# Attention's scaling of z ahead of its addition to x, with two buffers for the scaled z

## The chip, the cores and the metric

The kernel runs on one core of one Trainium2 chip, as one program. The metric is the device time of one execution in microseconds; the median of 3 runs is given. Engines are named as in the profile: PE is TensorE (PEld its weight loads), DVE is VectorE, ACT is ScalarE, POOL is GpSimd, SP is the engine whose queue issues the DMAs (SPq).

## What is computed

A block of three layers on x of 16 x 1024 x 256 in float32: half an FFN with weights and activations quantised to FP4 in blocks of 16, linear attention with 16 heads, and the same half FFN again.

```python
x = x + 0.5 * ffn(layernorm(x), w_gate, w_up, w_down)
x = x + attn(layernorm(x), Wqkv, bqkv, Wout, bout, gamma, beta)
x = x + 0.5 * ffn(layernorm(x), w_gate, w_up, w_down)

# in attn, after q, k, v: causal linear attention through cumulative sums
num = einsum('blhe,blhef->blhf', q, cumsum(k v)); den = einsum('blhe,blhe->blh', q, cumsum(k)) + eps
z = (num / den) @ Wout.T + bout
return (z - mean(z)) / sqrt(var(z) + 1e-5) * gamma + beta
```

The change touches the last line and the addition of its result to x.

## The kernel before

x stays in SBUF (x_sb) for the whole kernel, as N = 128 tiles of 128 rows (partitions) by 256 columns. Three stages pass over the tiles: the first FFN, attention, and the second FFN. Each engine has a program of its own, and they meet only through semaphores: `ready(engine, name, t)` waits until the step called name is done for tile t, `freed(...)` until a buffer's last reader is done. Each engine issues its instructions strictly in the order in which the step function writes them. In all stages the work is skewed: in step i an engine works on several tiles at once, each at another point of its way. The order of work on an engine is thus written out by hand, and nothing reorders it.

Attention is run for steps i = -4 to 131. Steps 5 to 120 are a loop on each engine, whose body holds four steps (`ATTN_TURN = 4`), so 29 passes. The first steps are interleaved with the first FFN's last, the last ones with the second FFN's first.

What one step of attention does, as far as it matters here (names are those in the trace, with their line):

- TensorE: q and k (ps_qk, L1265) of tile i+1 from xT, a transpose of k (L1273), v (L1278), the numerator of tile i-1 (ps_num, L1297 and L1302), the scores of tile i (L1310), the sums k v of tile i (L1321), and the projection z of tile i-2 (ps_z; L1330 the bias, L1333 the rest). ps_z has one buffer: L1330 waits for z_gamma, the increment of zg.
- VectorE: statistics of x for tile i+4 (L1053) and of z for tile i-3 (L1059), the masked scores (L1063), the two aggregations (L1072 for z, L1074 for x, both into mv), the addition to x for tile i-4 (L1079), the state before (L1085), zg for tile i-3 (L1091: z less its mean, times gamma), den (L1095, waits for num), feat (L1099), the reciprocal (L1102), o (L1108), and the states second and first (L1113, L1120).
- GpSimd: k_eo (L1148, L1149, waits for feat), the lower half of o (L1153, o_split), the state mid (L1160), the lower half of the normalised x (L1164), 1/sqrt of both variances (L1175 adds eps, L1177 is the power -0.5, on two columns: one for x, one for z; L1175 waits for both aggregations), the shift (L1181), and beta added to x_sb (L1183).
- ScalarE: among others the upper half of o (L1192) and the normalised x (L1240, L1244).
- SP: it issues oT's transpose (L1034) after o_split and then xT's transpose (L1040) after x_split, always in this order; xT feeds L1265 two steps later on its tile.

So the addition of tile i-4 uses the zg that VectorE wrote in the step before. zg is one buffer of 128x256 float32 at 13376 bytes into the stage area. z's 1/sqrt(var) comes from GpSimd between the two.

In the first FFN two lines serve below as a measure: L714 on VectorE (128x16, reads two tensors in SBUF) and L791 on GpSimd (128x704, reads SBUF).

Of the kernel before, what the change touches and what calls it, by code (L numbers as in the profile page):

```python
# [31 lines left out]
ALU = mybir.AluOpType  # L32
# [4 lines left out]
P = 128  # L37
D = 256
# [31 lines left out]
def column(ap, t):  # L70
    return ap[:, bass.ds(t, 1)]


def valid(t, n):
    return not isinstance(t, int) or 0 <= t < n
# [45 lines left out]
def macaron(nc, x, wqkv, bqkv, wout, bout, gamma, beta, wg, wu, wd, out):  # L121
# [6 lines left out]
    with ExitStack() as whole:  # L128
# [27 lines left out]
        def at(name, offset, shape, dt=F32):  # L156
# [9 lines left out]
        of_ffn_0, of_ffn_1 = [ffn(nc, ffn_sems, attn_sems, at, N, half, x_sb, x_t, out_t, wgu_hi, wgu_lo, wd_hi, wd_lo, unscale,  # L166
                                  minus_half, eps, minus_one, offsets, x_loaded, attn_added, stored) for half in range(2)]
        of_attn_steps = attention(nc, attn_sems, at, N, x_sb, A, ident, minus_half, eps, ffn_sems, attn_added, sem("attn_set_up"))
        block = whole.enter_context(nc.Block())

# [740 lines left out]
def attention_constants(sbuf, N):  # L911
    def sb(name, shape, dt=F32):
# [5 lines left out]
                     sb("feat_eps", [P, 1]), sb("keep", [P, N]))  # L918


ATTN_PLACES = {"o": 8352, "oT": (1024, 2048), "o_hl": (9376, 4096), "mid": (5632, 6176), "before": (6720, 7264), "first": 7808, "second": 11264, "k_nat": 12352, "zg": 13376,
               "k_eo": (15104, 17152), "scores": 19200, "v_nat": (23296, 24384), "v_eo": (25472, 27648), "q_feat": (29824, 30848), "q_rows": (31872, 33920),
               "expo": (35968, 38016), "xT": (40064, 41088), "x_hl": (42112, 43136), "xn": 44160,
               "bn6": 45184, "z_bn6": 45216, "mv": (45248, 45280), "rstd": (45376, 45408), "shift": (45440, 45472),
# [3 lines left out]
def attention(nc, S, at, N, x_sb, A, ident, minus_half, eps, F, attn_added, set_up):  # L928
    unscale, o_scale, one, rows, causal, diag, even, odd, of_pair, of_pair_eps, eps2, own, ones3, bout3, feat_eps, keep = (
        A.unscale, A.o_scale, A.one, A.rows, A.causal, A.diag, A.even, A.odd, A.of_pair, A.of_pair_eps, A.eps2, A.own, A.ones3, A.bout3, A.feat_eps, A.keep)  # L930
    with ExitStack() as scope:
        def sb(name, shape, dt=F32):
            return at("attn_" + name, ATTN_PLACES[name], shape, dt)

        def pair(name, shape, dt=F32):
            return [at(f"attn_{name}{j}", ATTN_PLACES[name][j], shape, dt) for j in range(2)]

        def psum(name, shape, dt=F32):
            return scope.enter_context(nc.psum_tensor("attn_" + name, shape, dt))
# [3 lines left out]
        mv = pair("mv", [P, 4])  # L943
        rstd = pair("rstd", [P, 2])
# [8 lines left out]
        k_nat = sb("k_nat", [P, D])  # L953
# [5 lines left out]
        first, second = sb("first", [P, DC, PAIRS, VW]), sb("second", [P, DC, PAIRS, VW])  # L959
        mid = pair("mid", [P, DC, PAIRS, VW])  # L960
        before = pair("before", [P, DC, PAIRS, VW])
        den, rden = sb("den", [P, HEADS]), sb("rden", [P, HEADS])
        o = sb("o", [P, D])
        o_hl = pair("o_hl", [P, 2 * D], F16)
        oT = pair("oT", [P, 2 * DC, P], F16)
        z_bn6 = sb("z_bn6", [P, 6])
        zg = sb("zg", [P, D])

        ps_qk = psum("ps_qk", [P, 2 * DC, P])
        ps_kT_first = psum("ps_kT_first", [P, 512])  # L970
# [3 lines left out]
        ps_z = psum("ps_z", [P, 512])  # L974

        def ready(eng, name, t, k=1, per=1):
            eng.wait_ge(S[name], t * per + k)
# [23 lines left out]
        def by_head(ap):  # L1001
            return ap.rearrange("p c k w -> p (c k) w")
# [40 lines left out]
        def vector_step(dve, i, par):  # L1043
            oth = 1 - par
            ts, tf, tm, tz, ta = i + 4, i + 1, i - 1, i - 3, i - 4
# [26 lines left out]
                nc.vector.bn_aggr(mv[oth][:, 2:4], z_bn6[:]).then_inc(S["z_stats"], 1)  # L1072
            if valid(ts, N):
                nc.vector.bn_aggr(mv[par][:, 0:2], bn6[:]).then_inc(S["stats"], 1)  # L1074
            if valid(ta, N):
                ready(dve, "x_beta", ta)
                dve.wait_ge(S["rstd"], ta + 7)
                ready(dve, "z_gamma", ta)
                nc.vector.scalar_tensor_tensor(x_sb[:, ta, :], zg[:], rstd[par][:, 1:2], x_sb[:, ta, :], ALU.mult, ALU.add).then_inc(attn_added, 1)  # L1079
            if valid(i, N) and not (isinstance(i, int) and i == 0):  # L1080

                ready(dve, "mid", tm)
                ready(dve, "kv_second", tm)
                freed(dve, "num_done", i, 2)
                nc.vector.scalar_tensor_tensor(by_head(before[par][:]), by_head(mid[oth][:]), column(keep, i), by_head(second[:]), ALU.mult, ALU.add).then_inc(S["before"], 1)  # L1085
            if valid(tz, N):

                ready(dve, "z_stats", tz)
                if valid(ta, N):
                    dve.wait_ge(attn_added, ta + 1)  # L1090
                nc.vector.scalar_tensor_tensor(zg[:], ps_z[:, 0:D], mv[oth][:, 2:3], rows[:, 1, :], ALU.subtract, ALU.mult).then_inc(S["z_gamma"], 1)  # L1091
            if valid(tm, N):

                ready(dve, "num_done", tm)
# [156 lines left out]
        def tensor_step(pe, i, par):  # L1251
# [72 lines left out]
            if valid(to, N):  # L1324
# [9 lines left out]
                last.then_inc(S["proj_done"], 1)  # L1334

        return Programs(sync_step, vector_step, gpsimd_step, scalar_step, tensor_step)


# [208 lines left out]
```

## Time and profile before

| | |
|---|---|
| median of 3 runs | 2185.19 us (2185.08 to 2187.68) |
| profiled execution, its own time | 2185.49 us |
| its span, first to last instruction | 2183.1 us |
| mean granted TensorE clock | 0.994 |
| busy, share of the span | PE 96%, DVE 94%, ACT 88%, POOL 87% |
| attention's loop | about 800 to 1410 us of the span |

Busy shares are averages over stages. Matmuls are pipelined and their ends are modelled in the trace, so short stalls of TensorE are better seen from the times at which its steps begin than from its busy time. "Idle before <-releaser" says who let an engine go on.

### The profile page before, as it was taken

To read this page: it belongs to the slowest core of one execution; us is meant where nothing else is said; L and a number is where in the kernel's file an instruction comes from. 1 tells how busy PE (TensorE), PEld (TensorE's weight loads), DVE (VectorE), ACT (ScalarE), POOL (GpSimd) and SP (SyncE) were. 2 spreads that over 40 slices of the span, in tenths; PEclk is the share of its full clock that TensorE was granted. 3 is DMA by queue.
4 is the path that set the end of the run, shared out by engine and by line. 5 is a ranking of instruction groups with operands and counts; after the bars stand their busy time and mean duration, and the time that the engine had idled before them with its cause. 6 is when DMAs were issued, how large, how long until landed. Compare 5 with 4: busy or idle time off the path is not lost.

```text
span 2183.1 us, 90488 instructions
## 1 busy us (share of the span) xinstructions
PE 2100.8 (96%) x30384; PEld 1503.3 (69%) x30384; DVE 2044.3 (94%) x5231; ACT 1926.2 (88%) x4136; POOL 1907.3 (87%) x3002
## 2 busy tenths in 40 slices
PE   3899999999999999999999999969999999999998
PEld 1566666666666688888888888855666666666665
DVE  7999999999999789999999999979999999999997
ACT  7888888888888789999999999978988888888885
POOL 5999999999999778888888888868999999999996
PEclk9999999999999999999999999989999999999999
DMA  4665555555555432222232222224555555555555
GB/s 103 131 125 115 116 115 116 115 115 115 114 114 108 84 58 61 61 61 61 61 62 62 61 61 61 62 44 76 120 116 114 114 114 114 114 115 115 115 118 118
DMA packets 719855, 208.72 MB, mean 96 GB/s; under 512 B 666400, under 2 KB 719520, under 8 KB 719776
## 3 DMA queue, kind: packets, MB, share of 16 engines
q1 hardware_dynamic: 719776, 207.76, 46.6%
q8 instruction: 39, 0.64, 0.1%
q14 instruction: 40, 0.33, 0.1%
HBM read 20.38 MB, written 16.78 MB: 17 GB/s over the span
## 4 chain that ended last, share of the span: by engine, by line
PE 89%; issue 3%; POOL 3%; DVE 3%; DMA 1%; ACT 1%; SPq 1%; POOLq 0%; DVEq 0%; ACTq 0%
PE ffn_ps_gu L861 39%; PE ffn_ps_down L873 20%; PE attn_ps_qk L1265 8%; PE attn_ps_sc L1310 5%; PE attn_ps_num L1297 4%; PE attn_ps_v_second L1278 4%; PE attn_ps_z L1333 3%; PE attn_ps_num L1302 2%; PE attn_ps_kT_first L1273 1%; PE attn_ps_z L1330 1%; PE attn_ps_kT_first L1321 1%; DMA attn_xT<-attn_x_hl 1%; POOL ffn_h_hl L791 1%; DMA x_sb<-in_L_ffn_w_up 0%; POOL ffn_h_hl L792 0%
## 5 line engine op out<-in xcount | busy, mean ns | idle before, releaser
L861 PE MATMUL ffn_ps_gu<-wgu_hi,ffn_xT 128*128 128x512 f16 (+1 forms) x3072 | 737.7, 363 | 18.4 <-DVE ffn_hx L710 8.0
L861 PEld LDWEIGHTS ffn_ps_gu<-wgu_hi,ffn_xT 128*128 128x128 f16 x3072 | 300.7, 98 | 304.7 <-issue 22.3
L861 PE MATMUL ffn_ps_gu<-wgu_lo,ffn_xT 128*128 128x512 f16 (+1 forms) x1536 | 431.0, 362 | 0.0
L791 POOL TENSOR_TENSOR ffn_h_hl<-ffn_q,ffn_h_scale_hi 128x704 f16<-128x704 f16 x256 | 352.4, 1376 | 28.0 <-DVE ffn_q L751 8.6
L807 ACT ACTIVATE ffn_quarter<-ffn_y,offsets 128x960 int16<-128x960 f32 (+2 forms) x264 | 282.5, 1070 | 99.3 <-DVE ffn_y L759 96.9
L873 PE MATMUL ffn_ps_down<-wd_hi,ffn_hT 128*128 128x256 f16 x2816 | 349.3, 273 | 8.1 <-DVE x_sb L735 4.2
L792 POOL TENSOR_TENSOR ffn_h_hl<-ffn_q,ffn_h_scale_lo 128x704 f16<-128x704 f16 x256 | 355.1, 1387 | 0.0
L873 PEld LDWEIGHTS ffn_ps_down<-wd_hi,ffn_hT 128*128 128x128 f16 x2816 | 274.6, 98 | 68.8 <-issue 7.1
L721 DVE TENSOR_REDUCE ffn_per_block<-ffn_hx 128x60 f32<-128x960 f32 (+2 forms) x264 | 298.1, 1129 | 5.3
L759 DVE TENSOR_TENSOR ffn_y<-ffn_hx,ffn_per_block 128x960 f32<-128x960 f32 (+2 forms) x264 | 292.6, 1108 | 0.0
L843 ACT ACTIVATE ffn_odd<-ffn_quarter,offsets 128x960 f16<-128x960 int16 (+2 forms) x264 | 278.8, 1056 | 10.8 <-POOL ffn_shift L786 10.8
L802 ACT ACTIVATE ffn_silu<-ffn_ps_gu,unscale 128x704 f32<-128x704 f32 x256 | 215.5, 842 | 73.6 <-PE ffn_ps_gu L861 71.5
L861 PEld LDWEIGHTS ffn_ps_gu<-wgu_lo,ffn_xT 128*128 128x128 f16 x1536 | 150.7, 98 | 155.0 <-issue 1.9
L710 DVE SCALAR_TENSOR_TENSOR ffn_hx<-ffn_ps_gu,unscale,ffn_silu 128x704 f32<-128x704 f32 x256 | 240.9, 941 | 17.0 <-PE ffn_ps_gu L861 13.3
L777 POOL TENSOR_TENSOR ffn_x_hl<-ffn_q,ffn_x_scale_hi 128x256 f16<-128x256 f16 x256 | 158.1, 617 | 73.4 <-DVE ffn_q L751 59.4
L873 PE MATMUL ffn_ps_down<-wd_lo,ffn_hT 128*128 128x256 f16 x1536 | 209.5, 273 | 0.0
L1265 PE MATMUL attn_ps_qk<-attn_xT,attn_w_hi 128*128 128x128 f16 x2048 | 178.8, 219 | 8.0 <-DMA attn_xT<-attn_x_hl 5.4
L873 PEld LDWEIGHTS ffn_ps_down<-wd_lo,ffn_hT 128*128 128x128 f16 x1536 | 150.3, 98 | 17.4
L782 POOL TENSOR_TENSOR ffn_x_hl<-ffn_q,ffn_x_scale_lo 128x256 f16<-128x256 f16 x256 | 161.6, 631 | 0.0
L1063 DVE TENSOR_TENSOR attn_scores<-attn_ps_sc,attn_causal 128x1024 f32<-128x1024 f32 x128 | 154.3, 1205 | 0.0
L845 ACT ACTIVATE ffn_hx<-x_sb,ffn_shift,ffn_rstd 128x256 f32 (+1 forms) x256 | 150.0, 586 | 1.5 <-POOL ffn_shift L786 1.5
L1265 PEld LDWEIGHTS attn_ps_qk<-attn_xT,attn_w_hi 128*128 128x128 f16 x2048 | 136.0, 98 | 22.2 <-DMA attn_xT<-attn_x_hl 16.8
(184 smaller groups left out, 5246.3 us busy)
## 6 DMA issues: line engine op xcount, KB each, us to landing
x_sb<-in_L_attn_x SPq DMA_DIRECT2D x128, 128.0 KB, 2.4
out<-x_sb SPq DMA_DIRECT2D x128, 128.0 KB, 2.1
attn_v_eo<-attn_v_nat SPq DMA_DIRECT2D x256, 34.0 KB, 1.8
ffn_xT<-ffn_x_hl SPq DMA_TRANSPOSE x256, 2.5
ffn_hT<-ffn_h_hl SPq DMA_TRANSPOSE x256, 3.5
attn_xT<-attn_x_hl SPq DMA_TRANSPOSE x128, 2.4
attn_oT<-attn_o_hl SPq DMA_TRANSPOSE x128, 2.5
x_sb<-in_L_ffn_w_gate SPq DMA_DIRECT2D x2, 352.0 KB, 5.0
```

The costliest lines, as they stand in the source:

```text
L710: nc.vector.scalar_tensor_tensor(hx[par][:, 0:INNER], ps_gu[par][:, INNER:2 * INNER], unscale[:, 1:2], silu[:], ALU.mult, ALU.mult).then_i ...
L721: nc.vector.tensor_reduce(amax[:, blocks_in(front)], blocks(hx[par][:, front]), AXX, ALU.max, apply_absolute_value=True).then_inc(S["amax" ...
L759: nc.vector.tensor_tensor(blocks(y[:, front]), blocks(hx[par][:, front]), over_block(inv[:, at], at.stop - at.start), ALU.mult).then_inc(S ...
L782: nc.gpsimd.tensor_tensor(blocks(x_hl[par][:, D:]), blocks(q[par][:, INNER:]), over_block(x_scale_lo[par][:], XB), ALU.mult).then_inc(S["x ...
L791: nc.gpsimd.tensor_tensor(blocks(h_hl[par][:, 0:INNER]), blocks(q[par][:, 0:INNER]), over_block(h_scale_hi[par][:], HB), ALU.mult)
L792: nc.gpsimd.tensor_tensor(blocks(h_hl[par][:, INNER:]), blocks(q[par][:, 0:INNER]), over_block(h_scale_lo[par][:], HB), ALU.mult).then_inc ...
L802: nc.scalar.activation(silu[:], ps_gu[par][:, 0:INNER], ACT.Silu, scale=unscale[:, 0:1]).then_inc(S["silu"], 1)
L807: nc.scalar.activation(quarter[:, back], y[:, back], ACT.Identity, bias=offsets[:, 0:1], scale=4.0 / HALF_MIN).then_inc(S["quarter"], 1)
L843: nc.scalar.activation(odd[:, back], quarter[:, back], ACT.Identity, bias=offsets[:, 1:2], scale=HALF_MIN / 4.0).then_inc(S["odd"], 1)
L861: last = nc.tensor.matmul(ps_gu[par][:, a:b], xT[par][:, c, :], w[:, k, a:b], start=(n == 0), stop=(n == len(terms) - 1))
L873: last = nc.tensor.matmul(ps_down[:, 0:D], hT[par][:, c, :], w[:, c, :], start=(n == 0), stop=(n == len(terms) - 1))
L1265: last = nc.tensor.matmul(ps_qk[:, col, :], w[:, col, k], aT, start=(n == 0), stop=(n == len(terms) - 1))
```

## The change

zg becomes a pair of buffers. The instruction that writes it (L1091) moves ahead of the addition (L1079) and of before (L1085). In step i it writes `zg[oth]`, and the addition reads `zg[par]`, which the step before wrote. Two waits go: the addition's for z_gamma, and zg's for the addition (attn_added). No instruction is added or dropped. The second buffer lies at 3072 bytes, in space that attention didn't use. Lines behind the place have numbers that are 3 lower in the changed kernel; zg becomes L1078, the addition L1082, before L1088.

```diff
-ATTN_PLACES = {..., "zg": 13376,
+ATTN_PLACES = {..., "zg": (13376, 3072),
...
-        zg = sb("zg", [P, D])
+        zg = pair("zg", [P, D])
...
                 nc.vector.bn_aggr(mv[par][:, 0:2], bn6[:]).then_inc(S["stats"], 1)
+            if valid(tz, N):
+
+                ready(dve, "z_stats", tz)
+                nc.vector.scalar_tensor_tensor(zg[oth][:], ps_z[:, 0:D], mv[oth][:, 2:3], rows[:, 1, :], ALU.subtract, ALU.mult).then_inc(S["z_gamma"], 1)
             if valid(ta, N):
                 ready(dve, "x_beta", ta)
                 dve.wait_ge(S["rstd"], ta + 7)
-                ready(dve, "z_gamma", ta)
-                nc.vector.scalar_tensor_tensor(x_sb[:, ta, :], zg[:], rstd[par][:, 1:2], x_sb[:, ta, :], ALU.mult, ALU.add).then_inc(attn_added, 1)
+                nc.vector.scalar_tensor_tensor(x_sb[:, ta, :], zg[par][:], rstd[par][:, 1:2], x_sb[:, ta, :], ALU.mult, ALU.add).then_inc(attn_added, 1)
             if valid(i, N) and not (isinstance(i, int) and i == 0):
                 ...
                 nc.vector.scalar_tensor_tensor(by_head(before[par][:]), ...).then_inc(S["before"], 1)
-            if valid(tz, N):
-
-                ready(dve, "z_stats", tz)
-                if valid(ta, N):
-                    dve.wait_ge(attn_added, ta + 1)
-                nc.vector.scalar_tensor_tensor(zg[:], ps_z[:, 0:D], mv[oth][:, 2:3], rows[:, 1, :], ALU.subtract, ALU.mult).then_inc(S["z_gamma"], 1)
```

VectorE's order in one of the four steps of attention's loop, before (the numbers behind names are the program's buffers):

```order
L1074 BN_AGGR attn_mv_136<-attn_bn_135 128x2
L1079 ISA [waits attn_z_gamma,attn_rstd,attn_x_beta]
L1079 SCALAR_TENSOR_TENSOR x_sb<-attn_zg,attn_rstd_138,x_sb 128x256
L1085 SCALAR_TENSOR_TENSOR attn_before_165<-attn_mid_164,attn_keep,attn_second 128x136 [waits attn_num_done,attn_kv_second,attn_mid]
L1091 SCALAR_TENSOR_TENSOR attn_zg<-attn_ps_z,attn_mv_137,attn_rows 128x256 [waits attn_added,attn_z_stats]
L1095 TENSOR_SCALAR attn_den<-attn_ps_num,attn_o_scale 128x16 [waits attn_num_done]
```

And the same step in the changed kernel:

```order
L1074 BN_AGGR attn_mv_136<-attn_bn_135 128x2
L1078 SCALAR_TENSOR_TENSOR attn_zg_176<-attn_ps_z,attn_mv_137,attn_rows 128x256 [waits attn_z_stats]
L1082 ISA [waits attn_rstd,attn_x_beta]
L1082 SCALAR_TENSOR_TENSOR x_sb<-attn_zg_175,attn_rstd_138,x_sb 128x256
L1088 SCALAR_TENSOR_TENSOR attn_before_165<-attn_mid_164,attn_keep,attn_second 128x136 [waits attn_num_done,attn_kv_second,attn_mid]
L1092 TENSOR_SCALAR attn_den<-attn_ps_num,attn_o_scale 128x16 [waits attn_num_done]
```

zg has moved up by two operations, its only wait is the one for the aggregation, and den now follows before. The other engines' orders are the same in both kernels.

## Rows read from the trace of the kernel before

**Rows 1.** The page, busy us (share of the span) x instructions

```profile
PE 2100.8 (96%) x30384; PEld 1503.3 (69%) x30384; DVE 2044.3 (94%) x5231; ACT 1926.2 (88%) x4136; POOL 1907.3 (87%) x3002
```

**Rows 2.** Windows: stretch, length, busy by engine, granted clock, DMA share, GB/s

```profile
820.00:1410.00 590.00, 588.47 (x18183) 526.38 (x18180) 542.08 (x1522) 571.58 (x1305) 506.48 (x978) 1.00 0.30 61
```

**Rows 3.** Waits, 820 to 1410 us: us in total, times, longest

```profile
PEld attn_ps_qk L1265 <- DMA attn_xT<-attn_x_hl: 7.4, 27, 0.3
...
DVE attn_den L1095 <- PE attn_ps_num L1302: 39.4, 109, 0.5
...
POOL attn_k_eo L1148 <- DVE attn_expo L1099: 15.8, 53, 0.3
```

**Rows 4.** Timeline of weight loads: start, us, instruction, idle before

```profile
1110.64 0.29 PEld L1265 LDWEIGHTS attn_ps_qk<-attn_xT,attn_w_hi 128*128 128x128 f16 x4
...
1115.40 0.10 PEld L1330 LDWEIGHTS attn_ps_z<-attn_bout,attn_ones 128*128 128x128 bf16 x1
...
1116.13 0.26 PEld L1265 LDWEIGHTS attn_ps_qk<-attn_xT,attn_w_hi 128*128 128x128 f16 x4
...
1121.63 0.23 PEld L1265 LDWEIGHTS attn_ps_qk<-attn_xT,attn_w_hi 128*128 128x128 f16 x4 [0.28 <-DMA attn_xT<-attn_x_hl]
...
1132.36 0.25 PEld L1265 LDWEIGHTS attn_ps_qk<-attn_xT,attn_w_hi 128*128 128x128 f16 x4
```

**Rows 5.** Timeline of SP's queue, step k1

```profile
1117.67 1.20 SPq L1034 DMA_TRANSPOSE attn_oT<-attn_o_hl  x1
1119.13 1.19 SPq L1040 DMA_TRANSPOSE attn_xT<-attn_x_hl  x1
```

**Rows 6.** Timeline of GpSimd, step k0 into k1

```profile
1113.32 0.27 POOL L1175 TENSOR_TENSOR attn_rstd<-attn_mv,attn_eps 128x2 f32<-128x2 f32 x1 [0.29 <-DVE attn_mv L1072]
1113.67 0.70 POOL L1177 TENSOR_TENSOR attn_rstd<-attn_rstd,minus_half 128x2 f32<-128x2 f32 x1
...
1114.80 0.73 POOL L1183 TENSOR_TENSOR x_sb<-x_sb,attn_rows 128x256 f32 x1
1115.63 0.48 POOL L1148 TENSOR_SCALAR attn_k_eo<-attn_expo,attn_even 128x256 f32<-128x256 f32 x1
1116.20 0.48 POOL L1149 TENSOR_SCALAR attn_k_eo<-attn_expo,attn_odd 128x256 f32<-128x256 f32 x1
1116.77 0.67 POOL L1153 TENSOR_TENSOR attn_o_hl<-attn_o,attn_o_hl 128x256 f16<-128x256 f32 x1
```

**Rows 7.** Timeline of VectorE, step k0

```profile
1112.93 0.17 DVE L1072 BATCH_NORM_AGGREGATE attn_mv<-attn_z_bn 128x2 f32<-128x6 f32 x1
...
1113.08 0.45 DVE L1079 SCALAR_TENSOR_TENSOR x_sb<-attn_zg,attn_rstd,x_sb 128x256 f32 x1
1113.45 0.35 DVE L1085 SCALAR_TENSOR_TENSOR attn_before<-attn_mid,attn_keep,attn_second 128x136 f32<-128x136 f32 x1
1113.73 0.48 DVE L1091 SCALAR_TENSOR_TENSOR attn_zg<-attn_ps_z,attn_mv,attn_rows 128x256 f32<-128x256 f32 x1
1114.43 0.23 DVE L1095 TENSOR_SCALAR attn_den<-attn_ps_num,attn_o_scale 128x16 f32<-128x16 f32 x1 [0.23 <-PE attn_ps_num L1302]
...
1115.24 0.24 DVE L1102 RECIPROCAL attn_rden<-attn_den 128x16 f32<-128x16 f32 x1
1115.51 0.42 DVE L1108 TENSOR_TENSOR attn_o<-attn_ps_num,attn_rden 128x256 f32<-128x256 f32 x1
```

**Rows 8.** Timeline of ScalarE, step k1

```profile
1116.20 0.40 ACT L1192 ACTIVATE attn_o_hl<-attn_o 128x256 f16<-128x256 f32 x1
```

**Rows 9.** Timeline of GpSimd in attention's first steps, no addition beside it

```profile
770.99 0.19 POOL L1175 TENSOR_TENSOR attn_rstd<-attn_mv,attn_eps 128x2 f32<-128x2 f32 x1
771.26 0.71 POOL L1177 TENSOR_TENSOR attn_rstd<-attn_rstd,minus_half 128x2 f32<-128x2 f32 x1
```

**Rows 10.** Timelines of VectorE and GpSimd in the first FFN, two places

```profile
549.03 0.17 DVE L714 TENSOR_TENSOR ffn_x_scale_lo<-ffn_scale,ffn_x_scale_hi 128x16 f32<-128x16 f32 x1
...
549.02 1.41 POOL L791 TENSOR_TENSOR ffn_h_hl<-ffn_q,ffn_h_scale_hi 128x704 f16<-128x704 f16 x1
...
695.74 1.38 DVE L714 TENSOR_TENSOR ffn_x_scale_lo<-ffn_scale,ffn_x_scale_hi 128x16 f32<-128x16 f32 x1
...
695.72 1.38 POOL L791 TENSOR_TENSOR ffn_h_hl<-ffn_q,ffn_h_scale_hi 128x704 f16<-128x704 f16 x1
```

**Rows 11.** Timeline of VectorE in attention's last steps

```profile
1467.20 0.48 DVE L1079 SCALAR_TENSOR_TENSOR x_sb<-attn_zg,attn_rstd,x_sb 128x256 f32<-128x256 f32 x1
1467.79 0.48 DVE L1091 SCALAR_TENSOR_TENSOR attn_zg<-attn_ps_z,attn_mv,attn_rows 128x256 f32<-128x256 f32 x1
```

More of the change, by code:

```diff
@@ L918, in attention_constants @@
                      sb("feat_eps", [P, 1]), sb("keep", [P, N]))
-ATTN_PLACES = {"o": 8352, "oT": (1024, 2048), "o_hl": (9376, 4096), "mid": (5632, 6176), "before": (6720, 7264), "first": 7808, "second": 11264, "k_nat": 12352, "zg": 13376,
+ATTN_PLACES = {"o": 8352, "oT": (1024, 2048), "o_hl": (9376, 4096), "mid": (5632, 6176), "before": (6720, 7264), "first": 7808, "second": 11264, "k_nat": 12352, "zg": (13376, 3072),
                "k_eo": (15104, 17152), "scores": 19200, "v_nat": (23296, 24384), "v_eo": (25472, 27648), "q_feat": (29824, 30848), "q_rows": (31872, 33920),
```

## Prediction

> **What bounds the kernel now.** I read the page's busy line first: TensorE is busy for 96% of the span [rows 1]. Then the stage that the change touches, attention's loop, in a row of the windows view: from 820 to 1410 us TensorE is busy for 588.5 of 590 us at a granted clock of 1.00, so at 2.4 GHz [rows 2]. That busy time hides stalls, as the times of the steps show. One pass of the loop on every engine does four tiles ("a turn", steps k0 to k3), and there are 29 turns. In the timeline of weight loads k0 begins at 1110.64, k1 at 1116.13 and k2 at 1121.63, and the next k0 at 1132.36: 21.72 us a turn, 5.43 a step [rows 4]. Ahead of k2 the loads stood 0.28 us for the transpose that makes xT; the view of waits counts 27 of these, 7.4 us, one in each turn [rows 2 to 4]. So once a turn TensorE is bound by whoever makes xT late.
>
> Follow it back. k2's xT was issued on SP at 1119.13, right behind oT's, which began at 1117.67 and keeps SP until 1118.87 [rows 5]. oT waits for GpSimd's o_split (L1153), which ran from 1116.77 to 1117.44 [rows 6]. ScalarE's half of it was ready at 1116.60, earlier than GpSimd's own last operation, which ended at 1116.68 [rows 6, 8]. So GpSimd held it up. GpSimd runs without a wait from 1113.32 on, where L1175 starts once VectorE has written the statistics: L1175, L1177 (the power), the shift, L1183, then k_eo at 1115.63, 0.10 after L1183's end and so not waiting for VectorE's feat [rows 6]. **What GpSimd loses between 1113.32 and 1115.6 in k0, TensorE loses at k2**, once in each turn.
>
> VectorE is not the bound here: before each den (L1095) it waits for TensorE's num, 39.4 us over 109 times, 0.23 us of it in this k0 [rows 3, 7].
>
> **The change, part by part.** No instruction is added or dropped. Three things happen.
>
> (1) zg (L1091, 0.48 us) goes ahead of the addition (L1079) and of before (L1085). It also frees ps_z for TensorE sooner, but that frees nothing: in k0 zg ended at 1114.21, and the bias matmul that waits for it loads at 1115.40 [rows 4, 7]. Price 0.
>
> (2) The wait of zg for the addition goes, and the addition's wait for zg is now on one of the step before. Neither wait was a stall in the loop, since before lay between them: it is 1113.45 to 1113.80, and zg starts at 1113.73 [rows 7]. What comes instead is a wait of zg for the statistics of L1072, which end at 1113.10 [rows 7]. For a VectorE operation that waits for the last one the rows show a start 0.03 us behind its end (L1102 ends at 1115.48, L1108 starts at 1115.51) [rows 7], and at the most 0.11 (the addition ends at 1467.68, zg starts at 1467.79) [rows 11]. I take 0.03: zg's new wait is the only one on it, and the 0.11 stood behind two. So zg starts at 1113.13, where the addition started at 1113.08: 0.05 us longer a step, and 0.13 at most. The idle 0.23 before den takes either [rows 7]. Price 0 for VectorE; without that idle it would be 128 times 0.05, 6.4 us.
>
> (3) The addition moves past GpSimd's L1175 and onto L1177. This is what I price, since the two engines exclude each other. In the first FFN, VectorE's L714, which takes 0.17 us, started 0.02 us after GpSimd's L791 and then took 1.38, as long as L791 itself. Where it started only 0.01 after, it took 0.17 and L791 took 1.41 rather than 1.38 [rows 10]. So the first to start has it (up to 0.01 us apart VectorE wins), and the other waits. L714 reads two tensors in SBUF; so do the addition (zg, x_sb) and before (mid, second). zg reads PSUM and one tensor in SBUF. Now look at L1175 in k0: the addition ends at 1113.53 and L1175 at 1113.59, 0.27 long, where the same operation with no addition beside it took 0.19 [rows 6, 7, 9]. So the addition gives way 0.13 us ahead of its recorded end (1113.59 less 0.19 is 1113.40), and L1175 had lost 0.08.
>
> The Trainium skill has this as a rule, in "SBUF — State Buffer", section "Who interferes with whom": a VectorE instruction with two SBUF inputs and a GpSimd instruction that reads SBUF keep each other out for the whole instruction, by order of start. The rows agree but for the end: held to the addition's full end, the sum below would be 0.31 us a turn, 9.0 over the loop.
>
> After the change, in k0: L1175 starts at 1113.32 as before, is free, and ends at 1113.51. L1177 follows L1175's start by 0.27 when free (770.99, 771.26) [rows 9], so it starts at 1113.59. zg, from 1113.13, takes 0.48, and the next operation starts 0.08 ahead of an end (before, 0.35 long, to zg: 1113.45 to 1113.73) [rows 7]: the addition starts at 1113.53, 0.06 us ahead of L1177, and so goes first. It takes 0.45 when nothing holds it [rows 7], ends at 1113.98 and gives way at 1113.85. L1177's own 0.70 (0.71 when nothing was near) [rows 6, 9] then ends at 1114.55, where it ended at 1114.37: **0.18 us later**. All that follows on GpSimd up to o_split moves by it, and k2's xT wait goes from 0.28 to 0.46. In k1 the same clash puts L1177 at one place relative to the statistics, so the delay isn't added a second time; in about half the steps (53 of them, 15.8 us) GpSimd waits for VectorE's feat at k_eo anyway, 0.3 us a time, and the delay goes into that [rows 3].
>
> Sum: 29 turns by 0.18 is 5.2 us. The last few steps of attention outside the loop have the same two operations and GpSimd on the chain; three by 0.18, 0.5 us, is an estimate. Together 5.7. The profiled execution took 2185.49 (2183.1 of span and 2.4 around it), 0.3 above the median of 2185.19; from the median it is 2190.9.
>
> **The rivals.** (a) *GpSimd's power comes first.* If zg's wait costs 0.11, the addition starts at 1113.61, 0.02 behind L1177's 1113.59, and by L714's rows that is late enough. L1177 gets in, ends at 1114.29, 0.08 earlier than now, and k2's wait shrinks: 29 by 0.08, 2.3 us less, 2182.9. ScalarE's half, ready at 1116.60, would not allow more than about 0.1 [rows 8]. For it: a lead of only 0.06 in the forecast. Against it: the single wait. This one is not slower. Chance 0.12.
>
> (b) *zg's wait costs nothing*, since L1074 runs between: zg starts at 1113.08 where the addition did. Then all comes 0.05 earlier, the delay is 0.13, and 32 of them are 4.2: 2189.4. Against it: waiting operations start 0.03 behind an end, others 0.08 ahead of it [rows 7]. Chance 0.10. The Trainium skill says so in "VectorE: DVE Perf Modes", section "The DRAIN you can't avoid": a semaphore between VectorE operations costs nothing extra. The pair of rows doesn't bear it out for an operation that waits for the last one; with one between, no row here shows it.
>
> (c) *The delay has no effect.* The clash happens, but GpSimd's chain gives it back somewhere that I take for full, or L1177 reads late enough. 2185.2. Against it: L1175 has lost time in just this way, and 27 like waits in 590 us, one in each 21.7, are no chance [rows 2, 3]. Chance 0.15.
>
> (d) *The late start, VectorE still first.* With 0.10 for zg's wait the addition starts at 1113.60, which is 0.01 behind L1177 and by L714's rows still first; it gives way at 1113.92, and L1177 ends 0.25 later: 29 and 3 times 0.25, 8.0 us, 2193.2. I count it with the forecast, as its upper end.
>
> (e) *VectorE becomes late.* before, now last, starts at 1113.90 with L1177 inside. If the power kept VectorE out until 0.13 ahead of its end, 1114.42, before would end at 1114.77, and den, 0.08 ahead of that, start at 1114.69, 0.26 late. It decides from where den's lateness is more than scores has to spare before TensorE's num; each 0.1 us that comes through in 116 steps is 11.6 us, so 2202.5 with the forecast's 5.7. Against it: the power reads two columns only. Chance 0.08.
>
> **The numbers.** The forecast, with (d), has 0.55, and (a) 0.12. A change under 0.2%, 4.4 us, is about what can't be told from none; slower needs 2189.6 or more, which the forecast reaches six times in seven (0.47), and (e) too: 0.55. Faster by 4.4 us has no mechanism but scatter: 0.03. The rest is 0.42. The range from 2184.5 to 2193.5 takes in (b), (c), the forecast and (d), and leaves out (a) and (e), 0.20.
>
> **What would show it.** After, in k0: L1175 near 0.19 us, not 0.27, in all steps; L1177 about 1.0 long rather than 0.70, its end about 0.13 before plus 0.70 behind the addition's; the addition at 0.45; DMA waits ahead of k2 about 0.46, some 13 us in sum; den's idle still over zero; turns of 21.90 us. Wrong if L1177 keeps 0.70 and the turn 21.72, or if turns shrink.

## The result, and the profile of the changed kernel

The changed kernel took 2189.32 us, median of 20 executions (2185.77 to 2191.93), beside 2184.27 us for the kernel before in 20 (2178.59 to 2188.12): a ratio of 1.0025, with an interval of 1.0019 to 1.0031. By the ratio that is 5.5 us slower, 4.2 to 6.8; the two medians lie 5.1 apart. The forecast was 5.7 us slower.

The page of the changed kernel's profiled execution (2189.1 us, span 2186.3), and its row of windows for the same 590 us as in [rows 2]:

```profile
PE 2103.0 (96%) x30384; PEld 1501.2 (69%) x30384; DVE 2052.3 (94%) x5231; ACT 1922.7 (88%) x4136; POOL 1913.0 (87%) x3002
```

```profile
820.00:1410.00 590.00, 584.20 (x18106) 519.62 (x18107) 543.96 (x1514) 566.20 (x1299) 512.53 (x973) 1.00 0.30 61
```

The busy line looks like that of [rows 1], and the granted clock is 1.00 in the loop as it was [rows 2]. A change of 0.25% can't be seen in either. What can be seen is that TensorE's busy time in the window fell by 4.3 us, from 588.5. The waits of the same window (us in total, times, longest) say for what:

```profile
DVE attn_den L1092 <- PE attn_ps_num L1299: 32.0, 90, 0.7
...
PEld attn_ps_qk L1262 <- DMA attn_xT<-attn_x_hl: 18.7, 54, 0.5
...
POOL attn_k_eo L1145 <- DVE attn_expo L1096: 8.0, 27, 0.4
```

Line numbers here are 3 lower from den (L1092, once L1095) on, since the diff makes the file shorter: L1172 is what was L1175, and so on. Weight loads stand 18.7 us for xT where they stood 7.4 [rows 3], and GpSimd's waits for feat (the tile attn_expo) have halved, from 53 to 27 (15.8 us to 8.0). Where the first comes from is seen in one turn. VectorE in k0, to be laid beside [rows 7]:

```profile
1114.32 0.17 DVE L1072 BATCH_NORM_AGGREGATE attn_mv<-attn_z_bn 128x2 f32<-128x6 f32 x1
1114.41 0.15 DVE L1074 BATCH_NORM_AGGREGATE attn_mv<-attn_bn 128x2 f32<-128x6 f32 x1
1114.52 0.48 DVE L1078 SCALAR_TENSOR_TENSOR attn_zg<-attn_ps_z,attn_mv,attn_rows 128x256 f32<-128x256 f32 x1
1114.92 0.48 DVE L1082 SCALAR_TENSOR_TENSOR x_sb<-attn_zg,attn_rstd,x_sb 128x256 f32 x1
1115.32 0.35 DVE L1088 SCALAR_TENSOR_TENSOR attn_before<-attn_mid,attn_keep,attn_second 128x136 f32<-128x136 f32 x1
1115.82 0.23 DVE L1092 TENSOR_SCALAR attn_den<-attn_ps_num,attn_o_scale 128x16 f32<-128x16 f32 x1
```

GpSimd in the same step and into k1, beside [rows 6], and SP's two transposes behind it, beside [rows 5]:

```profile
1114.71 0.19 POOL L1172 TENSOR_TENSOR attn_rstd<-attn_mv,attn_eps 128x2 f32<-128x2 f32 x1 [0.30 <-DVE attn_mv L1072]
1114.98 0.98 POOL L1174 TENSOR_TENSOR attn_rstd<-attn_rstd,minus_half 128x2 f32<-128x2 f32 x1
1116.16 0.27 POOL L1178 TENSOR_SCALAR attn_shift<-attn_mv,attn_rstd 128x1 f32<-128x1 f32 x1 [0.21 <-POOL attn_rstd L1174]
1116.39 0.73 POOL L1180 TENSOR_TENSOR x_sb<-x_sb,attn_rows 128x256 f32 x1
1117.21 0.48 POOL L1145 TENSOR_SCALAR attn_k_eo<-attn_expo,attn_even 128x256 f32<-128x256 f32 x1
...
1118.34 0.68 POOL L1150 TENSOR_TENSOR attn_o_hl<-attn_o,attn_o_hl 128x256 f16<-128x256 f32 x1
```

```profile
1119.26 1.21 SPq L1034 DMA_TRANSPOSE attn_oT<-attn_o_hl  x1
...
1120.72 1.19 SPq L1040 DMA_TRANSPOSE attn_xT<-attn_x_hl  x1
```

Put every time against the start of L1072 in its own step. Before, that was 1112.93, and the power ended at 1114.37, 1.44 later. Now it is 1114.32, and the power ends at 1115.96, 1.64 later: GpSimd has lost **0.20 us**. xT is issued 6.40 after it instead of 6.20 (1119.13 less 1112.93). The 0.20 arrives whole. The weight loads of the five step starts, beside [rows 4]:

```profile
1112.12 0.23 PEld L1262 LDWEIGHTS attn_ps_qk<-attn_xT,attn_w_hi 128*128 128x128 f16 x4 [0.23 <-DMA attn_xT<-attn_x_hl]
...
1117.50 0.28 PEld L1262 LDWEIGHTS attn_ps_qk<-attn_xT,attn_w_hi 128*128 128x128 f16 x4
...
1123.21 0.23 PEld L1262 LDWEIGHTS attn_ps_qk<-attn_xT,attn_w_hi 128*128 128x128 f16 x4 [0.46 <-DMA attn_xT<-attn_x_hl]
...
1128.43 0.30 PEld L1262 LDWEIGHTS attn_ps_qk<-attn_xT,attn_w_hi 128*128 128x128 f16 x4
...
1133.93 0.23 PEld L1262 LDWEIGHTS attn_ps_qk<-attn_xT,attn_w_hi 128*128 128x128 f16 x4 [0.23 <-DMA attn_xT<-attn_x_hl]
```

The wait ahead of k2 is 0.46 where it was 0.28, and k1 to k2 takes 5.71 where it took 5.50: 0.21 more. But k0 to k1 takes 5.38 where it took 5.49, and k2 to the next k0 10.72 where it took 10.73. The turn is 21.81 against 21.72. In this pair of traces, then, about 0.1 of the 0.2 us is given back within the turn, and a second wait for xT, 0.23 ahead of k0, has appeared (27 by 0.46 and 27 by 0.23 are the 18.7 us). The span is only 3.2 us longer here (2183.1 to 2186.3), less than the medians differ. That had to be explained too.

### The profile page after: what moved, and what is told of

Same layout as the page of the kernel before. It is cut to its first block, busy times and chain, and to the rows that moved or that the text cites. A ratio compares the mean times of both kernels' runs of the same rounds, so it can differ in the third digit from the quotient of the medians.

```text
span 2186.3 us, 90361 instructions
## 1 busy us (share of the span) xinstructions
PE 2103.0 (96%) x30384; PEld 1501.2 (69%) x30384; DVE 2052.3 (94%) x5231; ACT 1922.7 (88%) x4136; POOL 1913.0 (87%) x3002
## 4 chain that ended last, share of the span: by engine, by line
PE 73%; issue 7%; DVE 6%; POOL 5%; DMA 4%; SPq 2%; ACT 1%; DVEq 0%; POOLq 0%; ACTq 0%
PE ffn_ps_gu L861 39%; PE ffn_ps_down L873 21%; PE attn_ps_qk L1262 4%; DMA attn_xT<-attn_x_hl 4%; PE attn_ps_num L1294 2%; PE attn_ps_v_second L1275 2%; SPq L1034 2%; PE attn_ps_sc L1307 1%; POOL attn_rstd L1174 1%; PE attn_ps_num L1299 1%; POOL attn_o_hl L1150 1%; PE attn_ps_z L1330 1%; POOL attn_k_eo L1145 1%; PE attn_ps_kT_first L1270 1%; DVE attn_z_bn L1059 1%
## 5 line engine op out<-in xcount | busy, mean ns | idle before, releaser
L791 POOL TENSOR_TENSOR ffn_h_hl<-ffn_q,ffn_h_scale_hi 128x704 f16<-128x704 f16 x256 | 351.7, 1374 | 27.7 <-DVE ffn_q L751 8.4
```

The lines of the kernel that those rows point to most:

```text
L791: nc.gpsimd.tensor_tensor(blocks(h_hl[par][:, 0:INNER]), blocks(q[par][:, 0:INNER]), over_block(h_scale_hi[par][:], HB), ALU.mult)
```

## Experiments

Three questions. Is the loss from the clash of the addition with GpSimd's power (my theory), or from the order itself: the second buffer, zg's new wait, VectorE's later den (rivals)? Is it k0 alone that counts? And why do the turns of two traces not give the whole difference?

### The parts of the change, without the clash

Three kernels keep the two buffers and change only the order on VectorE. The changed kernel's order is zg, addition, before. First the old order with the new buffers (a diff against the kernel before; zg, still last, writes zg[oth] without its wait for the addition):

```diff
-        zg = sb("zg", [P, D])
+        zg = pair("zg", [P, D])
...
                 dve.wait_ge(S["rstd"], ta + 7)
-                ready(dve, "z_gamma", ta)
-                nc.vector.scalar_tensor_tensor(x_sb[:, ta, :], zg[:], rstd[par][:, 1:2], x_sb[:, ta, :], ALU.mult, ALU.add).then_inc(attn_added, 1)
+                nc.vector.scalar_tensor_tensor(x_sb[:, ta, :], zg[par][:], rstd[par][:, 1:2], x_sb[:, ta, :], ALU.mult, ALU.add).then_inc(attn_added, 1)
```

> Only the second buffer of zg, in the old order (addition, before, zg), without the two waits. Theory, that the clash of the addition with GpSimd's L1177 costs the time: nothing changes, L1177 ends 1.44 us after L1072's start in k0 as in the kernel before, turn 21.72 us, ratio 1.000. Rival, that the second buffer's place or the missing waits cost it: ratio about 1.002, turn 21.8.

Measured: 2185.28 us beside 2183.68, ratio 1.0009 (0.9998 to 1.0020), turn 21.68. The buffers and the dropped waits make no difference that is clear of noise, though the interval leaves room for up to 4 us.

The second kernel goes on from that one, with zg ahead of before but still behind the addition:

```diff
             if valid(ta, N):
...
+            if valid(tz, N):
+                ready(dve, "z_stats", tz)
+                nc.vector.scalar_tensor_tensor(zg[oth][:], ps_z[:, 0:D], mv[oth][:, 2:3], rows[:, 1, :], ALU.subtract, ALU.mult).then_inc(S["z_gamma"], 1)
             if valid(i, N) and not (isinstance(i, int) and i == 0):
...
-            if valid(tz, N):
-                ready(dve, "z_stats", tz)
-                nc.vector.scalar_tensor_tensor(zg[oth][:], ps_z[:, 0:D], mv[oth][:, 2:3], rows[:, 1, :], ALU.subtract, ALU.mult).then_inc(S["z_gamma"], 1)
```

> Two buffers, order addition, zg, before. Theory: the addition meets L1175 as in the kernel before, and zg, which reads one tensor in SBUF, is beside L1177; L1177 ends at 1.44 in k0, turn 21.72, ratio 1.000. Rival, that zg's move ahead of before (ps_z free sooner, before later) costs the time: ratio 1.002.

Measured: 2184.93 us, 1.0009 (0.9999 to 1.0018), turn 21.69. No difference from the kernel above: an earlier zg and an earlier free ps_z are worth nothing that shows. Both kernels read 1.0009, though, and their turns are 0.08 us over the shortest that was seen of the kernel before (21.60, below). So some 2 of the 5.5 us may belong to the pair of buffers and the dropped waits; this isn't shown.

The third has zg first, with its wait for the statistics, then before, then the addition:

```diff
             if valid(tz, N):
                 ready(dve, "z_stats", tz)
...
-            if valid(ta, N):
-                ready(dve, "x_beta", ta)
-                dve.wait_ge(S["rstd"], ta + 7)
-                nc.vector.scalar_tensor_tensor(x_sb[:, ta, :], zg[par][:], rstd[par][:, 1:2], x_sb[:, ta, :], ALU.mult, ALU.add).then_inc(attn_added, 1)
             if valid(i, N) and not (isinstance(i, int) and i == 0):
...
+            if valid(ta, N):
+                ready(dve, "x_beta", ta)
+                dve.wait_ge(S["rstd"], ta + 7)
+                nc.vector.scalar_tensor_tensor(x_sb[:, ta, :], zg[par][:], rstd[par][:, 1:2], x_sb[:, ta, :], ALU.mult, ALU.add).then_inc(attn_added, 1)
```

> Two buffers, order zg, before, addition. zg waits for the statistics as in the changed kernel, but before (0.35 us) is the one that stands on L1177's start. Theory: before starts at 0.61 and gives way at 0.83, so L1177 ends at 1.53, 0.09 later than before in k0; turn 21.72 to 21.81, ratio 1.000 to 1.001, between the two kernels. Rival, that zg's wait for the statistics costs the time: ratio 1.0025 as in the changed kernel.

Measured: 2185.35 us, 1.0005 (0.9997 to 1.0014), turn 21.70. Here before, which also reads two tensors in SBUF, lies on the power's start. Its timeline of GpSimd, and below it that of VectorE:

```profile
1112.05 0.20 POOL L1172 TENSOR_TENSOR attn_rstd<-attn_mv,attn_eps 128x2 f32<-128x2 f32 x1 [0.32 <-DVE attn_mv L1072]
1112.33 0.85 POOL L1174 TENSOR_TENSOR attn_rstd<-attn_rstd,minus_half 128x2 f32<-128x2 f32 x1
```

```profile
1111.87 0.48 DVE L1078 SCALAR_TENSOR_TENSOR attn_zg<-attn_ps_z,attn_mv,attn_rows 128x256 f32<-128x256 f32 x1
1112.27 0.35 DVE L1084 SCALAR_TENSOR_TENSOR attn_before<-attn_mid,attn_keep,attn_second 128x136 f32<-128x136 f32 x1
1112.54 0.48 DVE L1088 SCALAR_TENSOR_TENSOR x_sb<-attn_zg,attn_rstd,x_sb 128x256 f32 x1
```

before, 0.35 long, starts 0.06 ahead of the power and holds it for 0.15; the addition, 0.48 long, starts 0.06 ahead in the changed kernel and holds it for 0.28. The delay follows the length of what goes first: 0.35 less 0.15 is 0.20, and 0.48 less 0.28 is 0.20. The power ends 1.52 after L1072's start here, in the median of the loop, 0.08 later than before; 29 by 0.08 is 2.3 us, 0.1%, which the measured ratio can't tell from nothing. The changed kernel's loss isn't zg's place or its wait, for this kernel shares both.

### Take the clash away, keep the order

The changed kernel with the addition held back until GpSimd's first operation is done, so that the power has already begun:

```diff
                 dve.wait_ge(S["rstd"], ta + 7)
+                if valid(tz, N):
+                    dve.wait_ge(S["var"], i + 4)
                 nc.vector.scalar_tensor_tensor(x_sb[:, ta, :], zg[par][:], rstd[par][:, 1:2], x_sb[:, ta, :], ALU.mult, ALU.add).then_inc(attn_added, 1)
```

> The changed kernel, with the addition also waiting for L1172 (var), so that it starts just behind the power's start rather than just ahead. Theory: L1172 takes 0.19, the power 0.70, ending at 1.36 in k0, 0.08 earlier than in the kernel before and 0.28 earlier than in the changed one; turn 21.64 to 21.72, ratio to the kernel before 0.999 to 1.000. Rival, that the order zg first costs the time in itself: ratio 1.0025 or more, since a wait is added to VectorE.

Measured: 2184.30 us beside 2183.68, 1.0002 (0.9993 to 1.0011); the turn is 21.62. Its timelines of GpSimd and of VectorE:

```profile
1111.26 0.19 POOL L1174 TENSOR_TENSOR attn_rstd<-attn_mv,attn_eps 128x2 f32<-128x2 f32 x1 [0.36 <-DVE attn_mv L1072]
1111.53 0.70 POOL L1176 TENSOR_TENSOR attn_rstd<-attn_rstd,minus_half 128x2 f32<-128x2 f32 x1
```

```profile
1111.71 0.48 DVE L1084 SCALAR_TENSOR_TENSOR x_sb<-attn_zg,attn_rstd,x_sb 128x256 f32 x1 [0.15 <-issue]
1112.11 0.35 DVE L1090 SCALAR_TENSOR_TENSOR attn_before<-attn_mid,attn_keep,attn_second 128x136 f32<-128x136 f32 x1
1112.38 0.23 DVE L1094 TENSOR_SCALAR attn_den<-attn_ps_num,attn_o_scale 128x16 f32<-128x16 f32 x1
```

This kernel does more waiting than the changed one on VectorE (the addition starts about 0.24 us later after the statistics), and den has no recorded wait before it in this step. Yet the loss is gone, with the power back at its 0.70, though buffers and order are the changed kernel's. That settles it against every rival that blames VectorE's order or lateness. It also shows that the exclusion is one-sided here. The addition starts 0.18 us into the power and still takes 0.48, as with nothing held.

### Take the clash away by reading PSUM

The same order as in the second kernel, with a single zg that lies in a free half of z's PSUM bank instead of in SBUF, so that the addition reads one SBUF tensor only. The single buffer keeps the old waits, and zg starts at 0.71 after L1072's start instead of 0.52. Of its edit against the kernel before, the place of zg:

```diff
-        zg = sb("zg", [P, D])
...
+        zg = ps_z[:, D:2 * D]
```

> The kernel before with the order addition, zg, before, and zg kept in the free half of ps_z's bank in PSUM, so that the addition reads one tensor in SBUF and no longer excludes GpSimd. Theory: L1175 takes 0.19 us, the power starts at 0.66 and ends at 1.36 in k0, 0.08 earlier than with the same order and zg in SBUF (1.44); turn 21.60 to 21.65 against 21.685 there. Rival, that L1175's and the power's lengths have another cause than the two SBUF operands (VectorE busy beside them): 1.44 and 21.68 stay.

Measured: 2182.80 us beside 2183.89, 0.9995 (0.9987 to 1.0004), turn 21.63. Its groups of GpSimd instructions (count, busy time, mean ns), and the same two groups of the changed kernel and of the old order with two buffers:

```profile
L1177 POOL TENSOR_TENSOR attn_rstd<-attn_rstd,minus_half 128x2 f32<-128x2 f32 x109 | 76.4, 701 | 8.5
...
L1175 POOL TENSOR_TENSOR attn_rstd<-attn_mv,attn_eps 128x2 f32<-128x2 f32 x109 | 21.3, 195 | 14.0 <-DVE attn_mv L1072 8.1
```

```profile
L1174 POOL TENSOR_TENSOR attn_rstd<-attn_rstd,minus_half 128x2 f32<-128x2 f32 x109 | 101.1, 927 | 8.5
...
L1172 POOL TENSOR_TENSOR attn_rstd<-attn_mv,attn_eps 128x2 f32<-128x2 f32 x108 | 21.1, 195 | 8.1 <-DVE attn_mv L1072 8.1
```

```profile
L1174 POOL TENSOR_TENSOR attn_rstd<-attn_rstd,minus_half 128x2 f32<-128x2 f32 x109 | 76.5, 702 | 8.5
...
L1172 POOL TENSOR_TENSOR attn_rstd<-attn_mv,attn_eps 128x2 f32<-128x2 f32 x108 | 34.8, 322 | 10.4 <-DVE attn_mv L1072 10.0
```

With the addition on L1172 that one pays (322 ns instead of 195). With the addition on the power the power pays (927 instead of 702). With zg in PSUM neither does, though the addition is where it was and as long as it was (0.45). So it is the second SBUF operand that holds GpSimd. Run once more, in another set:

> The kernel with zg in PSUM once more, to learn whether its 0.9995 is a gain: theory (turn 0.05 to 0.09 shorter than the kernel before, 29 turns) says 1.5 to 2.6 us, ratio 0.9988 to 0.9993; if it is scatter, 1.000.

Measured: 2180.63 us beside 2182.56, 0.9990 (0.9981 to 1.0000). The two together speak for 1 to 2 us less than the kernel before; each interval still touches or holds 1, and the turns (21.63, 21.64) lie between the two that the kernel before has in its traces (21.72, 21.60), so I don't claim it as shown. Against the changed kernel the gain is plain.

### Where the tie lies, and which step counts

The addition starts only 0.06 ahead of the power, so a slight push should turn the order round. I put operations of one column, 0.06 us long, on VectorE ahead of the addition. First one:

```diff
             if valid(ta, N):
...
+                nc.vector.memset(spare[:], 0.0)
```

> The changed kernel with one more VectorE instruction, a memset of one column, between zg and the addition. It moves the addition from 0.61 to about 0.67 or 0.68, which in k0 is just behind the power's start at 0.66. Theory: in k0 the power goes first and ends at 1.36 rather than 1.64; where the power starts at 0.68 or later VectorE still goes first and L1174 ends even later (1.70). As k0 is what counts, the turn falls from 21.82 to 21.6 to 21.75: more work on VectorE and less time. Rival, that VectorE's lateness costs the time: turn 21.82 or more.

Measured: 2188.99 us beside 2183.89, 1.0025 (1.0017 to 1.0034). Nothing turned: the power still takes 0.99, and the loss is that of the changed kernel to the digit. A filler costs the operation behind it 0.01 us at the most. Then two:

```diff
             if valid(ta, N):
...
+                nc.vector.memset(spare[:, 0:1], 0.0)
+                nc.vector.memset(spare[:, 1:2], 0.0)
```

> As with one filler, but two memsets of one column each: the addition starts at about 0.74, behind the power's start in all four steps. Theory: the power is 0.70 long and ends near 1.38 in all steps, turn 21.60 to 21.65, ratio to the kernel before 0.999 to 1.000 and about 0.0025 under the changed kernel. Rival, VectorE's lateness: 21.82 or more.

Measured: 2185.29 us, 1.0006 (0.9997 to 1.0014), turn 21.68 (21.60 to 21.65 was expected). GpSimd's rows of k0 and of k1, and VectorE's two additions in them:

```profile
1113.33 0.19 POOL L1175 TENSOR_TENSOR attn_rstd<-attn_mv,attn_eps 128x2 f32<-128x2 f32 x1 [0.30 <-DVE attn_mv L1073]
1113.60 0.70 POOL L1177 TENSOR_TENSOR attn_rstd<-attn_rstd,minus_half 128x2 f32<-128x2 f32 x1
...
1118.54 0.19 POOL L1175 TENSOR_TENSOR attn_rstd<-attn_mv,attn_eps 128x2 f32<-128x2 f32 x1
1118.81 0.98 POOL L1177 TENSOR_TENSOR attn_rstd<-attn_rstd,minus_half 128x2 f32<-128x2 f32 x1
```

```profile
1113.57 0.51 DVE L1085 SCALAR_TENSOR_TENSOR x_sb<-attn_zg,attn_rstd,x_sb 128x256 f32 x1
...
1118.76 0.48 DVE L1085 SCALAR_TENSOR_TENSOR x_sb<-attn_zg,attn_rstd,x_sb 128x256 f32 x1
```

I had looked for the order to turn in all four steps. It turned in k0 alone (in 26 of 27), where the addition's lead is about 0.04; in k1 to k3, where it is 0.05 to 0.1, the power still pays 0.24 to 0.28. That is the best experiment of the set, by luck. VectorE has two operations more in every step, three steps of four still carry the clash, and the loss is all but gone (the turn is 0.14 us shorter than the changed kernel's). **What GpSimd loses in k0 is nearly all that counts**, as step (3) had it.

It isn't quite all. These are the loads of k2 and k3 in this kernel:

```profile
1121.57 0.23 PEld L1265 LDWEIGHTS attn_ps_qk<-attn_xT,attn_w_hi 128*128 128x128 f16 x4 [0.17 <-DMA attn_xT<-attn_x_hl]
...
1127.08 0.23 PEld L1265 LDWEIGHTS attn_ps_qk<-attn_xT,attn_w_hi 128*128 128x128 f16 x4 [0.32 <-issue]
```

With k0 free, TensorE stands 0.32 us ahead of k3 in each turn, for the xT that hangs on GpSimd's power in k1 as k2's hangs on the power in k0. The turn is about 0.065 us longer than that of the kernel with the addition held back, where no step carries the clash; that is 1.9 us over 29 turns, and the two times (1.0006 and 1.0002) can't tell it from nothing. The steps without a listed wait aren't far from one either. In every step of the loop, in all thirteen traces, the first of these loads starts 1.29 to 1.40 us behind the end of xT's issue, waited for or not, and the first matmul at most 0.11 us behind the load. So xT is early by about 0.1 us at the most, an estimate from these distances.

### Delay GpSimd directly

The kernel before, with one small operation on GpSimd between the power and the shift:

```diff
+                nc.gpsimd.memset(z_spare[:], 0.0)
```

> The kernel before, with one memset of one column on GpSimd between the power and the shift in every step; VectorE's program is untouched. Its length d is read from the trace, I expect 0.1 to 0.25 us. Theory: GpSimd's chain in k0 is what TensorE waits for, so a turn grows by most of d (with d of 0.2 by 0.1 to 0.2 us, ratio 1.001 to 1.0025). Rival, that GpSimd's delay is absorbed and the changed kernel's loss came otherwise: turn stays at 21.68 to 21.72, ratio 1.000.

Measured: 2187.68 us beside 2182.56, 1.0022 (1.0011 to 1.0033). GpSimd's timeline:

```profile
1113.61 0.70 POOL L1178 TENSOR_TENSOR attn_rstd<-attn_rstd,minus_half 128x2 f32<-128x2 f32 x1
1114.46 0.10 POOL L1182 MEMSET attn_z_spare<- 128x1 f32 x1 [0.15 <-POOL attn_rstd L1178]
1114.55 0.27 POOL L1183 TENSOR_SCALAR attn_shift<-attn_mv,attn_rstd 128x1 f32<-128x1 f32 x1
```

The operation mostly fills the 0.21 us for which the shift waits anyway: the shift starts 0.24 behind the power's end instead of 0.21. So the chain moved by 0.03 to 0.04 only, and 29 by 0.04 is 1.1 us. Measured were 4.8 (2.4 to 7.2). The sign agrees with the theory. The size doesn't, and the next two runs say part of why. So this run supports the sign alone.

### Both kernels once more

> The kernel before, profiled once more, to see how much a turn differs between two executions: 21.68 to 21.72 us if the 21.72 of its first trace is typical.

> The changed kernel, profiled once more: turn 21.82 us, L1174 ending at 1.64 in all four steps. Two theories of the 2 us between the loop's 2.9 and the measured 5 to differ: if it lies in single executions, this span or that of the kernel before will differ by 2 us from the first one with the same turn.

Measured, in one execution of each: 2180.16 us for the kernel before (span 2177.7) and 2186.39 for the changed one (span 2184.7). The turn of the changed kernel is 21.83, as before it was 21.81 to 21.82. The turn of the kernel before is 21.60, where its first trace had 21.72. The piece that differs is in k3. First two rows of TensorE from the first trace of the kernel before, then those from its second:

```profile
1129.31 0.88 PE L1297 MATMUL attn_ps_num<-attn_v_eo,attn_scores 128*32 128x34 f32 x64
1130.12 0.28 PE L1302 MATMUL attn_ps_num<-attn_before,attn_q_feat 64*64 64x68 f32 x2
```

```profile
1125.28 0.77 PE L1297 MATMUL attn_ps_num<-attn_v_eo,attn_scores 128*32 128x34 f32 x64
...
1125.98 0.28 PE L1302 MATMUL attn_ps_num<-attn_before,attn_q_feat 64*64 64x68 f32 x2
```

From the first row to the second is 0.81 us in one execution and 0.70 in the other, for the same 64 matmuls, and neither row has a wait on another engine. In the medians over the loop it is 0.85 and 0.70 in k3, and the same in k0 to k2 within 0.02. The two traces of the kernel before differ in their turn by 0.12 us, 3.6 us over 29 turns; the changed kernel has 0.70 there in both of its traces. That the two differences belong together is seen inside single executions. In the second trace of the kernel before 5 turns have a long k3 all the same, and the turns behind those take 21.70 us where the others take 21.57; the two kernels with two buffers and the old place of the addition, and the one with the addition held back, have one to three such turns each, with 0.12 to 0.16 us behind them. So the change costs 0.10 us a turn in the first pair of traces, where the kernel before has the long form, and 0.23 in the second, where it has the short one: 2.9 and 6.8 us over the loop, of the 3.2 and 7.0 by which the spans differ. The measured 5.5 lies between, as it should if the executions of the kernel before are of both kinds. That whole executions are was seen in two traces only. For the delayed kernel above the same would hold: its turn, 21.76, is 0.04 over the long form (the delay itself) and 0.16 over the short one. Why the 64 matmuls take one time or the other isn't settled. In k3 the short form is the commoner one in all eight traces of kernels with two buffers, and the long one in four of the five with one buffer; whether the buffers have to do with it no run here tests. A second thing is to be seen in this pair: the faster execution has more waiting for xT (10.2 us in 47 times, where the first trace has 7.4 in 27), for where TensorE is through the 64 sooner it stands 0.16 us for xT ahead of the next k0. The sum of a wait is no measure of what it costs.

## Why the prediction came out right, and where it was off

**Step (1), price 0.** Held, as far as noise lets one see. Moving zg ahead of before alone gave the same time as leaving it behind (2184.93 and 2185.28 us).

**Step (2), zg's wait.** Held. zg starts 0.20 after L1072's start, 0.11 after L1074's and 0.03 behind L1072's end (1114.49, 1114.52): the forecast's number. VectorE's idle before den took it. The wait counted 109 times [rows 3] is there 90 times now. So rival (b), in which the wait costs nothing, is out: a waiting operation starts 0.03 behind the end of the one it waits for, even with a third between, where one that doesn't wait starts 0.08 ahead of the end (1114.92 for zg's at 1115.00). The Trainium skill has in "VectorE: DVE Perf Modes", section "The DRAIN you can't avoid", that a semaphore between them costs nothing extra; the trace doesn't agree, by some 0.05 us a step.

**Step (3), the clash.** Held in mechanism, place and size. The forecast had the addition 0.06 ahead of the power (1114.92 and 1114.98: 0.06), L1175 back at 0.19 (195 ns over 108), the power near 1.0 (0.98) and its end 0.18 later (0.20). The 0.02 is the addition, which takes 0.48 behind zg, not the 0.45 that I took from its old place. The wait ahead of k2 was forecast at 0.46 and is 0.46. That the end is given up early was read rightly too: 1115.40, the addition's end, less 0.13, plus 0.70 is 1115.97, and the power ends at 1115.96. The rule of the Trainium skill ("SBUF — State Buffer", "Who interferes with whom") names the right pair of operations; by the "whole instruction" of the same page (section "SBUF: two separate sides") the power would have ended at 1116.10. What it doesn't tell is that the pair isn't symmetrical: see below.

**Only k0 counts.** Held in the main, shown by the kernel with two fillers; what k1 loses reaches TensorE at k3 once k0 is free, and is worth about 0.065 us a turn in the traces. The margin is narrower than the prediction has it. The other steps' delay went into GpSimd's waits for feat, as said: 53 of them before, 27 after.

**29 by 0.18, the sum.** Right in total, less tidy inside. The forecast's turn of 21.90 did not come: it is 21.82. Where the prediction multiplied k2's wait by 29 it took the rest of the turn as rigid, and it is not. In the changed kernel the 64 small matmuls take 0.70 us in k2 and k3, in the medians of the loop, where they had 0.75 and 0.85; part of what k2 lost is given back there, and in return a second wait for xT, 0.23 ahead of k0, opened (18.7 us of such waits, where I had said some 13). The sum came out at 5.5 nonetheless, because the trace that I started from has the long turn, 0.12 us over the one seen later. Against that trace alone I would have been 2.8 us too high (5.7 for 2.9). And up to some 2 us may belong to the two buffers, which the prediction had at nothing. So the agreement of 5.7 and 5.5 is partly fortune; the range would have held either.

**The last steps.** I added 0.5 us for attention's end, an estimate. Between the loop's end and attention's last operation the changed kernel loses 0.4 us in the first pair of traces and 0.1 in the second, and the steps in between differ by up to 0.8 within a pair. Nothing can be said of a term of that size.

**The rivals.** (a) is what the kernel with the held-back addition makes true: the power first, its end 0.07 earlier than before (1.37 after L1072's start, for 1.44). Its gain of 2.3 us did not show (1.0002). So an earlier GpSimd seems worth less than a later one costs. A likely reason, not tested, is that other things (ScalarE's half, feat) are then late next: GpSimd's waits for feat, 15.8 us before, are 17.9 in that kernel and 25.6 with zg in PSUM. (c), no effect, is out, as the ratio's interval begins at 1.0019. (d) needed a wait of 0.10 and got 0.03. (e), VectorE late, is out: before takes 0.35 and is not held at all.

## What to carry to other kernels

Before moving a VectorE operation with two SBUF operands, look at what GpSimd starts in the same tenths of a microsecond, and on whose chain that lies: a large operation that starts just ahead of a tiny one on GpSimd holds it until shortly before its own end (here 0.28 us of the addition's 0.48). Starting it a little later, or putting one of its operands in PSUM, makes the same order free. And when the change to be judged is a few tenths of a per cent, take two profiled executions of the kernel before: the one that the sum is made against may not be like the median.

## What I had not expected of the hardware

- The exclusion is one-sided between a large VectorE operation and a small GpSimd one. Behind the addition the power goes from 0.70 to 0.98 us; with the power first by 0.18, the addition takes the 0.48 that it takes anyway. It depends on the size of GpSimd's operation: in the first FFN L791, 1.38 us long on 128x704, holds VectorE's L714, 0.17 us long by itself, for as long as it lasts [rows 10]. Where between these two sizes it begins was not measured.
- VectorE gives way 0.13 to 0.14 us ahead of its recorded end at both of the lengths seen (0.35 and 0.48): the power's end less its 0.70. With one or two small operations queued ahead of the addition, a recorded lead of 0.05 us was enough for it to go first; with two, one of 0.04 was not.
- An operation of one column on VectorE is 0.06 us long in the record, and what follows it starts 0.01 us later.
- 64 matmuls of one shape, with nothing late and the same granted clock, take 0.70 or 0.85 us (medians of k3 in two executions). At the size of this change that is as large as the change.
